# Adding scaled expert rows to x in memory with accumulating scatters

## Chip, cores and metric

The kernel runs on one core of a Trainium2 chip. The metric is the device time of one execution in microseconds (us); for the kernel before, three runs gave 1421.79, 1427.64 and 1428.75, median 1427.64.

## Reference

Two transformer layers on x of shape 8 x 256 x 256 (2048 tokens of 256 values). Six sublayers follow each other, each as `x = layernorm(x + sublayer(x))`; only the last one, a mixture of eight experts with the two best per token, is touched:

```python
gate_scores = softmax(xf @ gate_w)                     # 2048 tokens, 8 experts
topk_scores, topk_idx = top_k(gate_scores, 2)
topk_scores = topk_scores / sum(topk_scores)           # the two shares
h = gelu(einsum('td,edf->etf', xf, w1) + b1)           # 256 -> 1024
y = einsum('etf,efd->etd', h, w2) + b2                 # 1024 -> 256
out = einsum('kt,ktd->td', topk_scores.T, y[topk_idx.T, tok])
x = layernorm(x + out)
```

## The kernel before

**Stages.** A and B (the first two attentions), C (a dense feed-forward), D and E (the second layer's attentions), F (the experts) and a last stage G, each over 8 batches of 256 tokens (two tiles of 128 rows). x stays in SBUF in x_tok. Each engine runs its own program; the order of the work is a list of steps made by in_rounds: an item (first, prio, name, args, at) puts its step k into round first + at[k], and within a round the item that began first comes first. All engines walk the same list and each takes the steps that are its own.

**Routing.** In stage E, at each batch's end (EFIN, SLOTS), the gate gives each token two experts, two shares (set_shares, into the tile shares) and two slots: expert times 2048 plus the token's rank within that expert. GpSimd scatters the token's row of x to x_slots at that slot, and its code (token number, plus 2048 for the second choice) to slot_codes, which was filled with "none" before. SyncE stores x_tok to x_rows as well.

**Experts.** A block is 256 slots of one expert. There are NBK = 23 blocks: the first block of each of the 8 experts, read from x_slots with plain loads, and 15 further blocks, whose expert and rows come from the counts; their weights are gathered by GpSimd (gather_weights, gather_x), three blocks ahead. Slots past an expert's count carry the code "none". Each block has four quarters q = 0 to 3 of its 1024 hidden values, so a round is a quarter, numbered n = 4j + q. Step 0 of a quarter: TensorE computes the hidden values (line 460 to 462 in product), ScalarE applies gelu (L1614) and casts the next weights (split_w, L1585, L1589), VectorE splits the results into a high and a low part (L2010, L2012, w_lo L1935, L1937), GpSimd splits half of the second weights (L761). Step 3: TensorE multiplies by the second weights (L1350), and in the last quarter VectorE adds the bias and leaves the block in yblock (L2021). Step 4, last quarter only: GpSimd scatters the block's 256 rows to y_rows at their codes (L790, two scatters of 128 rows); codes out of bounds are dropped. There are three yblock buffers.

**Codes.** At block 1, quarter 3 (CODES_AT) the codes of all blocks must be known. The last batch's codes are scattered by GpSimd in rounds 0 to 3 (L773); then come a load (first_codes) and a gather (more_codes), a cast of each on VectorE (row_codes, L1950), four transposes on TensorE (L468) and small VectorE steps that give slot_i and token_i.

**Last stage.** When all scatters have landed, SyncE loads y_rows back, two loads of 256 KB a batch (yc). For each batch b in GS, VectorE does four multiply-adds (L2033, share times y plus x) and the layernorm's statistics (ln_stats: L480, L485, L488) in round b, GpSimd a power (L494), VectorE in round b + 2 the scale (L499), ScalarE applies it to two tiles (ln_apply, L508), and SyncE stores the batch. ln_stats waits between L480 and L485 with `dve.wait_ge(s_x[fam], b - 1)`: batch b - 2 must have been applied, since two buffers are shared.

Of the kernel before, what the change touches and what calls it, by code (L numbers as in the profile page):

```python
# [53 lines left out]
def f(ap):  # L54

    return ap.bitcast(F32)
# [100 lines left out]
def f_steps():  # L157
    return in_rounds([(NQ * j + q, 0, "BLK", (j, q), 5 if q == NQ - 1 else 4) for j in range(NBK) for q in range(NQ)])
# [69 lines left out]
def build(nc, a, out):  # L228
    ctx, mid, early, late = ExitStack(), ExitStack(), ExitStack(), ExitStack()
    first_pieces, dw_scope, part, fpart, cpart = (ExitStack() for _ in range(5))  # L230
    with ctx:
# [44 lines left out]
        shares = sb("shares", [P, NT, TOPK])  # L276
# [3 lines left out]
        codes = sb("codes", [P, NT, TOPK], U32)  # L280
# [67 lines left out]
        s_const, s_rtmem, s_none, s_vz = sem("const"), sem("rtmem"), sem("none"), sem("vz")  # L348
# [58 lines left out]
        s_vone, s_shift = sem("ones"), sem("e_shift")  # L407
# [30 lines left out]
        block_codes = [sbf("first_codes", [NE, BT], U32), sbf("more_codes", [NMORE, BT], U32)]  # L438
        block_codes_f = [sbf("first_codes_f", [NE, BT]), sbf("more_codes_f", [NMORE, BT])]
        code_f, token_f = sbf("code_f", [P, BR * NBK]), sbf("token_f", [P, BR * NBK])  # L440
        slot_i, token_i = sbf("slot_i", [P, BR * NBK], U32), sbf("token_i", [P, BR * NBK], U32)
        fpart.close()
        ycs = [sb(f"yc{b}", [P, TOPK, TT, D], F32, cpart, "right") for b in range(B)]
        cpart.close()
# [4 lines left out]
        l_yc = [*((x, 64) for x in (*l_xt, *l_x)), *((x, 128) for x in l_ctx), (l_stage[0], 64), (l_stage[1], 80)]  # L449
# [115 lines left out]
        def set_shares(line, b):  # L565
            r = rt[b % 2]
            line.wait_ge(s_rs, b + 1)
            for t in range(TT):
                made = line.e.tensor_scalar(shares[:, b * TT + t, :], r[:, t, 2, 0:TOPK], r[:, t, 5, 3:4], 1.0, ALU.mult, ALU.mult)
            made.then_inc(s_sh, 1)  # L570
# [27 lines left out]
        def pool_program(pool):  # L598
# [20 lines left out]
            for v in vpad:  # L619
                pool.e.memset(v[:, :, :], 0.0).then_inc(s_vz, 1)  # L620
# [66 lines left out]
            for v in (v_d, *v_e):  # L687
                pool.mark(pool.e.memset(v[:, :, :, DH:32], 0.0))
                pool.wait_own()
                pool.e.memset(v[:, :, :, DH:DH + 1], 1.0).then_inc(s_vone, 1)  # L690
            for name, step, args in DE["pool"]:
# [33 lines left out]
                elif name == "SLOTS" and (args[0] < B - 1 or step < TT):  # L725
                    b, = args
                    pool.wait_ge(w_empty, 16 * (1 + NE))
# [1412 lines left out]
```

## Time and profile before

| | us |
|---|---|
| median of three runs | 1427.64 |
| the profiled execution | 1431.25 |
| its span | 1429.4 |
| TensorE busy | 1290.2 (90%) |
| VectorE busy | 915.3 (64%) |
| GpSimd busy | 730.1 (51%) |
| ScalarE busy | 572.9 (40%) |

In the page and the views PE is TensorE's matmuls, PEld its weight loads, DVE VectorE, ACT ScalarE, POOL GpSimd and SP SyncE; a q behind a name is the engine's queue of instructions. Busy time leaves out waiting and the issue of DMAs by SyncE. A share over the whole span is a mean over very different stages: the rows that matter are those of the expert loop (about 1105 to 1387 us) and of the last stage (1387 us to the end).

### The profile page before, as it was taken

What the parts mean: (1) busy time and instruction counts of PE and PEld (TensorE: products, weight loads), DVE (VectorE), ACT (ScalarE), POOL (GpSimd) and SP (SyncE); (2) the same over time, 40 slices, a digit from 0 to 9 for tenths busy, and PEclk for the clock granted to TensorE, in tenths of its full rate; (3) what the DMA queues carried; (4) which work ended last, traced back from release to release, by engine and by line L of the source; (5) the groups of instructions that cost most, each with busy time, mean ns of one, the idle gap of its engine ahead of it and who ended that gap; (6) DMA issues with size and microseconds to landing.
All of it is one profiled execution on the core that took longest, in us unless ns stands there. A gap on an engine that the chain in (4) does not pass through costs nothing.

```text
span 1429.4 us, 23660 instructions
## 1 busy us (share of the span) xinstructions
PE 1290.2 (90%) x9073; PEld 1098.9 (77%) x9073; DVE 915.3 (64%) x2305; ACT 572.9 (40%) x1172; POOL 730.1 (51%) x697
## 2 busy tenths in 40 slices
PE   6997999999999999999999989998773799999970
PEld 6996788888888888886777767776653799999970
DVE  3665622642272253235688878878765799999966
ACT  3567311121121121113545535544432576777732
POOL 3543566666576666634211242343434347888832
PEclk9998999999999999999999999999875899999995
DMA  6101223233343323310534343434713656666605
GB/s 188 36 22 35 74 89 108 91 115 91 118 133 96 96 88 104 92 62 25 155 93 132 90 81 117 97 88 131 232 43 110 190 198 224 222 231 233 229 18 168
DMA packets 63104, 169.56 MB, mean 119 GB/s; under 512 B 11029, under 2 KB 30735, under 8 KB 55056
## 3 DMA queue, kind: packets, MB, share of 16 engines
q1 hardware_dynamic: 52432, 122.19, 29.1%
q0 software_dynamic: 10560, 45.86, 9.1%
q8 instruction: 72, 1.18, 0.4%
q14 instruction: 40, 0.33, 0.1%
HBM read 138.57 MB, written 33.38 MB: 120 GB/s over the span
## 4 chain that ended last, share of the span: by engine, by line
PE 69%; DVE 16%; issue 4%; DMA 3%; ACT 3%; POOL 3%; SPq 1%; another core or an unknown queue 1%; ACTq 0%; POOLq 0%; DVEq 0%
PE bank L460 15%; PE bank L462 15%; PE bank L461 14%; PE bank L1350 6%; PE bank L468 5%; PE bank L1188 3%; PE bank L1107 3%; DVE shiftE L1873 2%; DVE shiftE L1867 2%; PE bank L1175 2%; PE bank L1266 1%; PE bank L1201 1%; DVE w_lo L1935 1%; DVE gh_hi L2010 1%; DVE x_tok L2033 1%
## 5 line engine op out<-in xcount | busy, mean ns | idle before, releaser
L1733 DVE CAST hid_hi<-bank 128x512 fp32r<-128x512 f32 x96 | 66.4, 691 | 254.9 <-ACT bank L1465 253.8
L602 POOL TENSOR_TENSOR wpiece_lo<-wraw,wpiece_hi 128x1024 fp32r<-128x1024 f32 x88 | 212.3, 2413 | 7.3
L462 PE MATMUL bank<-hid_hi,wpiece_hi 128*128 128x512 f32 x512 | 201.5, 394 | 0.0
L461 PE MATMUL bank<-hid_lo,wpiece_hi 128*128 128x512 f32 x512 | 200.2, 391 | 0.0
L460 PE MATMUL bank<-hid_hi,wpiece_lo 128*128 128x512 f32 x512 | 199.8, 390 | 0.0
L600 POOL TENSOR_SCALAR wpiece_hi<-wraw 128x1024 fp32r<-128x1024 f32 x88 | 93.9, 1067 | 154.4 <-PE bank L462 128.4
L1465 ACT ACTIVATE bank<-bank,ffn_scales 128x512 f32<-128x512 f32 x64 | 42.4, 662 | 304.4 <-PE bank L462 304.4
L461 PEld LDWEIGHTS bank<-hid_lo,wpiece_hi 128*128 128x128 f32 x512 | 96.1, 188 | 22.1
L460 PEld LDWEIGHTS bank<-hid_hi,wpiece_lo 128*128 128x128 f32 x512 | 96.1, 188 | 21.5 <-DVE hid_lo L1735 0.8
L462 PEld LDWEIGHTS bank<-hid_hi,wpiece_hi 128*128 128x128 f32 x512 | 96.2, 188 | 20.0
L460 PE MATMUL bank<-xgT_hi,w_lo 128*128 128x256 f32 x368 | 107.3, 292 | 1.8 <-DVE xgT_lo L1943 1.8
L1614 ACT ACTIVATE bank<-bank,w1raw 128x256 f32<-128x256 f32 x184 | 74.8, 447 | 85.3 <-PE bank L462 84.4
L461 PE MATMUL bank<-xgT_lo,w_hi 128*128 128x256 f32 x368 | 104.4, 284 | 0.0
L462 PE MATMUL bank<-xgT_hi,w_hi 128*128 128x256 f32 x368 | 104.3, 284 | 0.0
L1350 PE MATMUL bank<-w_hi,gh_lo 128*128 128x256 f32 x368 | 103.1, 280 | 0.0
L1350 PE MATMUL bank<-w_hi,gh_hi 128*128 128x256 f32 x368 | 102.8, 279 | 0.0
L1350 PE MATMUL bank<-w_lo,gh_hi 128*128 128x256 f32 x368 | 102.7, 279 | 0.0
L1867 DVE TENSOR_SCALAR_CACHE_REDUCE shiftE<-bank 128x256 f32<-128x256 f32 x256 | 92.9, 419 | 11.2 <-PE bank L1243 8.2
L468 PE MATMUL bank<-ident,shiftE 128*128 128x128 f32 x512 | 72.1, 284 | 24.1 <-DVE shiftE L1873 13.3
L761 POOL TENSOR_TENSOR w_lo<-w2raw,w_hi 128x256 fp32r<-128x256 f32 x92 | 76.4, 846 | 27.9 <-ACT w_hi L1589 27.1
L1873 DVE TENSOR_SCALAR shiftE<-shiftE,topE 128x256 f32<-128x256 f32 x256 | 86.9, 403 | 2.3
L1551 ACT ACTIVATE staging<-bank 128x512 f32<-128x512 f32 x128 | 69.5, 595 | 47.0 <-PE bank L468 38.5
(342 smaller groups left out, 3589.3 us busy)
## 6 DMA issues: line engine op xcount, KB each, us to landing
wraw<-in_C_w SPq DMA_DIRECT2D x88, 512.0 KB, 3.6
w2raw<-in_F_w SPq DMA_DIRECT2D x8, 1152.0 KB, 7.3
w1raw<-in_F_w SPq DMA_DIRECT2D x8, 1028.0 KB, 7.0
split_qk<-qk_hi SPq DMA_DIRECT2D x64, 128.0 KB, 2.7
xt_lo<-split_qk SPq DMA_DIRECT2D x8, 1024.0 KB, 4.8
xt_hi<-split_qk SPq DMA_DIRECT2D x8, 1024.0 KB, 5.3
split_qk<-qk_lo SPq DMA_DIRECT2D x32, 128.0 KB
split_qk<-ctx_raw SPq DMA_DIRECT2D x32, 128.0 KB, 2.4
```

Of the source, the lines that this page charges most:

```text
L460: pe.e.matmul(o, sl, mh, start=start and i == 0, stop=False)
L461: pe.e.matmul(o, sh, ml, start=False, stop=False)
L462: made = pe.e.matmul(o, sh, mh, start=False, stop=stop and i == n - 1)
L468: made = pe.e.transpose(dst, src, ident[0:n, 0:n])
L600: pool.mark(pool.e.tensor_scalar(pair[0], raw, 1.0, 0.0, ALU.mult, ALU.add))
L602: pool.e.tensor_tensor(pair[1], raw, f(pair[0]), ALU.subtract).then_inc(done, 1)
L761: pool.e.tensor_tensor(w2[n % 6][1][:, 1, :], w2_cols(*divmod(n, NQ))[:, 1, :], f(w2[n % 6][0][:, 1, :]), ALU.subtract).then_inc(s_w2lp, 1)
L1350: made = pe.e.matmul(u.ap[:, t * D:(t + 1) * D], hh[:, i, st], ww[:, i, :], start=fc == 0 and k == 0 and t == 0, stop=fc == FC - 1 and k == 2,
L1551: act.e.activation(prob_e[n % 3][:, i, :, :], u.ap[:, :].rearrange("p (k s) -> p k s", k=TT), ACT.Exp, scale=scale_e).then_inc(u.drained, 1)
L1614: made = act.e.activation(u.ap[:, cols], u.ap[:, cols], ACT.Gelu, bias=w1raw[j % 4][:, c:c + 1])
L1867: made = dve.e.tensor_scalar(shift_e[n % 3][:, m, :], scores[:, m, :], lim, -lim, ALU.min, ALU.max, accum_out=top[:, m:m + 1])
L1873: made = dve.e.tensor_scalar(sh, sh, -lim, top[:, m:m + 1], ALU.max, ALU.subtract)
```

## The change

The expert's rows are multiplied by their share while they are in yblock, and added to a copy of x in memory.

- The code of a slot becomes a pair, a mark: code and share. shares, codes and slot_codes give way to marks and slot_marks; set_shares writes into marks. The pairs are scattered, loaded and gathered as before, at twice the size, and the scatter waits for s_sh, the shares. "None" is filled in with two stores instead of one.
- row_codes casts codes and shares apart (four casts), TensorE transposes both (eight transposes), and VectorE makes share_f (the share of each row of each block), token_i, and row_out: the token's row in sum_rows, or a spare row behind the tokens (one for each partition and tile) for slots with no token.
- A new step 4 on ScalarE multiplies the block in place by its shares; step 5, the scatter, adds into sum_rows (compute_op=ALU.add) with no bounds check. Both steps stand 8 rounds behind the block's last quarter, where the scatter stood 4 behind it.
- The scatter of block j waits for the landing of that of block j - 1, since both may add to the same row; that of block 0 waits for the stores of x.
- SyncE stores each batch of x twice, to x_rows and to sum_rows.
- The last stage loads one sum a batch straight into x_tok, and VectorE's multiply-adds are gone.

```diff
 def f_steps():
-    ... "BLK", (j, q), 5 if q == NQ - 1 else 4) ...
+    ... "BLK", (j, q), (0, 1, 2, 3, 8, 8) if q == NQ - 1 else 4) ...
...
-        y_rows = nc.dram_tensor("y_rows", (TOPK * B * S, D), F32, kind="Internal").ap()
+        sum_rows = nc.dram_tensor("sum_rows", (B * S + BT, D), F32, kind="Internal").ap()
-        slot_codes = nc.dram_tensor("slot_codes", (NE * B * S + BT, 1), U32, kind="Internal").ap()
+        slot_marks = nc.dram_tensor("slot_marks", (NE * B * S + BT, 2), U32, kind="Internal").ap()
...
# pool_program
-                elif step == 4:
-                    u = use["F", "y", j]
+                elif step == 5:
                     pool.wait_ge(s_slots, 1)
-                    pool.wait_ge(u.drained, u.done)
+                    pool.wait_ge(s_shared, j + 1)
+                    if j:
+                        pool.wait_ge(w_y[(j - 1) % 3], 16 * BR * ((j - 1) // 3 + 1))
+                    else:
+                        for i in range(2):
+                            pool.wait_ge(w_rows[i], 16 * B)
                     for t in range(BR):
                         pool.e.indirect_dma_start(
-                            y_rows, bass.IndirectOffsetOnAxis(ap=slot_i[:, t * NBK + j:t * NBK + j + 1], axis=0),
-                            ysb[j % 3][:, t, :], None, bounds_check=TOPK * B * S - 1, oob_is_err=False).then_inc(w_y[j % 3], 16)
+                            sum_rows, bass.IndirectOffsetOnAxis(ap=row_out[:, t * NBK + j:t * NBK + j + 1], axis=0),
+                            ysb[j % 3][:, t, :], None, compute_op=ALU.add).then_inc(w_y[j % 3], 16)
...
# sync_program
-                    load(x_rows[b * S:(b + 1) * S, :]..., x_tok[:, b * TT:(b + 1) * TT, :], w_rows[b % 2])
+                    for rows in (x_rows, sum_rows):
+                        load(rows[b * S:(b + 1) * S, :]..., x_tok[:, b * TT:(b + 1) * TT, :], w_rows[b % 2])
...
             for b in range(B):
-                for k in range(TOPK):
-                    load(ycs[b][:, k, :, :], y_rows..., l_yc[b][0])
+                load(x_tok[:, b * TT:(b + 1) * TT, :], sum_rows[b * S:(b + 1) * S, :]..., l_sum[b][0])
...
# scalar_program
+                elif step == 4:
+                    u, marked = use["F", "y", j], use["F", "i"]
+                    act.wait_ge(marked.drained, marked.done)
+                    act.wait_ge(u.drained, u.done)
+                    for t in range(BR):
+                        y = ysb[j % 3][:, t, :]
+                        made = act.e.activation(y, y, ACT.Identity, scale=share_f[:, t * NBK + j:t * NBK + j + 1])
+                    made.then_inc(s_shared, 1)
...
# vector_program, row_codes
                 for k in range(2):
-                    dve.e.tensor_copy(block_codes_f[k][:, :], block_codes[k][:, :]).then_inc(s_codes, 1)
+                    dve.mark(dve.e.tensor_copy(block_marks_f[k][:, 0, :], block_marks[k][:, :, 0]))
+                    dve.e.tensor_copy(block_marks_f[k][:, 1, :], f(block_marks[k][:, :, 1])).then_inc(s_codes, 1)
...
# vector_program, last stage
                 if step == 0:
-                    dve.wait_ge(l_yc[b][0], l_yc[b][1] + 32)
-                    dve.wait_ge(s_x["E"], b + 1)
-                    dve.wait_ge(s_sh, B)
-                    for k in range(TOPK):
-                        dve.wait_own()
-                        for t in range(TT):
-                            n = b * TT + t
-                            made = dve.e.scalar_tensor_tensor(out=x_tok[:, n, :], in0=ycs[b][:, k, t, :], scalar=shares[:, n, k:k + 1],
-                                                              in1=x_tok[:, n, :], op0=ALU.mult, op1=ALU.add)
-                        dve.mark(made)
+                    dve.wait_ge(l_sum[b][0], l_sum[b][1] + 16)
                     ln_stats(dve, "C", B + b, x_tok[:, b * TT:(b + 1) * TT, :])
```

## Rows read from the trace of the kernel before

**Rows 1.** The page, busy time of each engine over the span.

```profile
PE 1290.2 (90%) x9073; PEld 1098.9 (77%) x9073; DVE 915.3 (64%) x2305; ACT 572.9 (40%) x1172; POOL 730.1 (51%) x697
```

**Rows 2.** Windows: stretch, length, busy of PE, PEld, DVE, ACT, POOL, clock, DMA share, GB/s.

```profile
1302.00:1313.60 11.60, 11.60 (x102) 11.60 (x101) 11.46 (x19) 8.12 (x17) 9.98 (x11) 1.00 0.64 239
```

**Rows 3.** Waits of PE, 1085 to 1392: who waited for whom, us, times, longest.

```profile
PE bank L468 <- DVE more_codes_f L1950: 8.7, 1, 8.7
```

**Rows 4.** Chain of waits up to the codes: start us, us, what.

```profile
1112.40 12.09 DMA slot_codes<-codes,slot
...
1125.37 6.88 DMA more_codes<-slot_codes,row_i
...
1132.34 0.28 DVE first_codes_f L1950
...
1132.88 0.60 PE bank L468 x4
```

**Rows 5.** Chain of waits behind the last matmul.

```profile
1386.50 0.70 DVE yblock L2021
...
1387.97 0.97 POOL y_rows L790
...
1389.24 2.10 DMA y_rows<-yblock,slot_i
...
1391.81 3.14 DMA yc<-y_rows
...
1394.97 0.89 DVE x_tok L2033 x2
```

**Rows 6.** Timeline of the last stage: start us, busy us, engine, line, operation [idle before].

```profile
1401.12 1.09 ACT L508 ACTIVATE x_tok<-x_tok,lnC_mv,lnC_rstd 128x256 f32<-128x256 f32 x2 [18.04 <-DVE lnC_mv L499]
...
1403.97 0.15 DVE L499 SCALAR_TENSOR_TENSOR lnC_mv<-lnC_mv,lnC_rstd 128x2 f32<-128x2 f32 x1
1404.04 1.79 DVE L2033 SCALAR_TENSOR_TENSOR x_tok<-yc,shares,x_tok 128x256 f32<-128x256 f32 x4
...
1404.16 1.09 ACT L508 ACTIVATE x_tok<-x_tok,lnC_mv,lnC_rstd 128x256 f32<-128x256 f32 x2 [1.95 <-DVE lnC_mv L499]
1405.86 0.75 DVE L480 BATCH_NORM_STATS2 lnC_stats<-x_tok 128x6 f32<-128x256 f32 x2
1406.65 0.25 DVE L485 BATCH_NORM_AGGREGATE lnC_mv<-lnC_stats 128x2 f32<-128x6 f32 x2
1406.93 0.17 DVE L488 TENSOR_SCALAR lnC_rstd<-lnC_mv 128x2 f32<-128x2 f32 x1
...
1419.37 2.07 ACT L508 ACTIVATE x_tok<-x_tok,lnC_mv,lnC_rstd 128x256 f32<-128x256 f32 x4 [1.95 <-DVE lnC_mv L499]
```

**Rows 7.** Timeline of ACT at the end of the loop.

```profile
1379.48 0.81 ACT L1614 ACTIVATE bank<-bank,w1raw 128x256 f32<-128x256 f32 x2 [1.97 <-PE bank L462]
```

**Rows 8.** Chain of waits ahead of the first block, 1085 to 1140.

```profile
1094.41 4.38 DMA x_slots<-x_tok,slot
1098.88 2.95 DMA xg<-x_slots
```

**Rows 9.** Timeline of DVE behind the codes.

```profile
1137.22 0.69 DVE L2010 CAST gh_hi<-bank 128x512 fp32r<-128x512 f32 x1 [2.72 <-issue]
```

**Rows 10.** Timelines of ACT and of DVE in a block's last quarter.

```profile
1312.24 0.81 ACT L1614 ACTIVATE bank<-bank,w1raw 128x256 f32<-128x256 f32 x2 [0.70 <-PE bank L462]
...
1314.20 0.69 DVE L2010 CAST gh_hi<-bank 128x512 fp32r<-128x512 f32 x1
```

**Rows 11.** Timeline of POOL over one block with gathers.

```profile
1304.47 1.28 POOL L790 DMA_INDIRECT y_rows<-yblock,slot_i  x1 [0.17 <-issue]
1306.06 0.98 POOL L790 DMA_INDIRECT y_rows<-yblock,slot_i  x1 [0.30 <-issue]
...
1311.70 0.96 POOL L739 DMA_INDIRECT w2raw<-in_F_w,wrow_i  x1 [0.35 <-DVE yblock L2021]
...
1316.11 1.28 POOL L790 DMA_INDIRECT y_rows<-yblock,slot_i  x1 [0.17 <-issue]
```

More of the change, by code:

```diff
@@ L229, in build @@
     ctx, mid, early, late = ExitStack(), ExitStack(), ExitStack(), ExitStack()
-    first_pieces, dw_scope, part, fpart, cpart = (ExitStack() for _ in range(5))
+    first_pieces, dw_scope, part, fpart = (ExitStack() for _ in range(4))
     with ctx:
@@ L279, in build @@
         seen = sb("seen", [P, NE], F32R)
-        codes = sb("codes", [P, NT, TOPK], U32)
+        marks = sb("marks", [P, NT, TOPK, 2], U32)
         block_no = sb("block_no", [P, NBK])
@@ L437, in build @@
         wrow_i = sbf("wrow_i", [P, NMORE], U32)
[L438 to L441, printed above, removed]
+        block_marks = [sbf("first_marks", [NE, BT, 2], U32), sbf("more_marks", [NMORE, BT, 2], U32)]
+        block_marks_f = [sbf("first_marks_f", [NE, 2, BT]), sbf("more_marks_f", [NMORE, 2, BT])]
+        code_f, token_f, share_f = (sbf(f"{n}_f", [P, BR * NBK]) for n in ("code", "token", "share"))
+        spare = sbf("spare", [P, BR])
+        row_out, token_i = sbf("row_out", [P, BR * NBK], U32), sbf("token_i", [P, BR * NBK], U32)
         fpart.close()
-        ycs = [sb(f"yc{b}", [P, TOPK, TT, D], F32, cpart, "right") for b in range(B)]
-        cpart.close()
         l_w1, l_w2 = ring(4, lambda i: sem(f"l_w1{i}")), ring(4, lambda i: sem(f"l_w2{i}"))
@@ L735, in pool_program @@
                         else:
-                            pool.e.indirect_dma_start(slot_codes, at, codes[:, b * TT + t, j:j + 1], None).then_inc(w_codes[b % 2], 16)
+                            pool.wait_ge(s_sh, b + 1)
+                            pool.e.indirect_dma_start(slot_marks, at, marks[:, b * TT + t, j, :], None).then_inc(w_codes[b % 2], 16)
             def gather(dst, rows, index, done):
@@ L778, in pool_program @@
                             pool.wait_ge(w_codes[i], 16 * 4 * (B // 2))
-                        gather(block_codes[1][:, :], slot_codes.rearrange("(r s) one -> r (s one)", s=BT), row_i[0:NMORE, 0:1], l_bc)
+                        gather(block_marks[1].rearrange("p s two -> p (s two)"), slot_marks.rearrange("(r s) two -> r (s two)", s=BT), row_i[0:NMORE, 0:1], l_bc)
                     if q == 2 and NE <= j + 3 < NBK:
@@ L831, in sync_program @@
                     load(iota8[:, :], a["iota8"], l_rt)
-                    load(codes[:, :, :], a["codes"], l_rt)
+                    load(marks[:, :, :, :], a["marks"], l_rt)
                     load(block_no[:, :], a["block_no"], l_rt)
@@ L837, in sync_program @@
                     sp.wait_ge(s_none, 1)
-                    load(slot_codes.rearrange("(p n) one -> p (n one)", p=P), none_t[:, :], w_empty)
+                    half = none_t.shape[1]
+                    for i in range(2):
+                        load(slot_marks.rearrange("(p n) two -> p (n two)", p=P)[:, i * half:(i + 1) * half], none_t[:, :], w_empty)
                 elif name == "CTX":
@@ L936, in sync_program @@
                         sp.wait_ge(w_codes[i], 16 * 4 * (B // 2))
-                    load(block_codes[0][:, :], slot_codes[0:NE * B * S].rearrange("(e s) one -> e (s one)", e=NE)[:, 0:BT], l_codes)
+                    load(block_marks[0][:, :, :], slot_marks[0:NE * B * S].rearrange("(e s) two -> e s two", e=NE)[:, 0:BT, :], l_codes)
                 first_weights(j)
@@ L1960, in row_codes @@
                 dve.e.tensor_scalar(token_i[:, :], token_f[:, :], float(B * S - 1), None, ALU.min).then_inc(s_tok, 1)
+                for t in range(BR):
+                    part = slice(t * NBK, (t + 1) * NBK)
+                    made = dve.e.tensor_scalar(row_out[:, part], token_f[:, part], spare[:, t:t + 1], None, ALU.min)
+                made.then_inc(s_slots, 1)
             for n in range(AHEAD - 1):
```

49 lines of the change are left out of this document (27 added, 22 removed).

## The prediction, written before the changed kernel ran

> **What bounds the kernel now.** I read the page first. TensorE is busy for 1290.2 of 1429.4 us [rows 1], so the question is whether the expert loop, which the change edits most, has room for more work. The windows of the loop say that TensorE has none to give: it is busy for all 11.60 us of a stretch as long as one block of 256 rows, at the full granted clock, with VectorE at 11.46, ScalarE at 8.12 and GpSimd at 9.98 [rows 2]. Work added there costs nothing as long as it does not make TensorE wait. Before the loop runs full there is one stall that bounds it: TensorE waits 8.7 us for the row codes in block 1 [rows 3]. It ends a chain in which the last scatter of codes lands 12.09 us after its issue starts, the gather of the codes takes 6.88, and a cast and four small transposes follow [rows 4].
>
> Behind the last matmul comes the tail, on which no TensorE work lies. In the chain of waits [rows 5] VectorE ends the last y block at 1387.20, GpSimd starts its two scatters at 1387.97 and 1389.24, the second has landed at 1391.34, the first loads at 1394.95. Then the last layernorm runs, batch by batch, at the pace of the ScalarE pairs in the timeline: 1401.12, 1404.16, so 3.04 us a batch [rows 6]. ScalarE ends at 1421.44 (1419.37 and 2.07). The rest, 8.0 us to the span's end, are the last stores and fixed steps; I leave it as it is.
>
> **The change, part by part.** The sum is against the profiled execution: 1431.25 us with a span of 1429.4. Its median neighbour is 1427.64, 3.6 lower (0.25%), and I add the difference to that. I call L the time from the start of the second scatter of a block to the landing of both.
>
> *Layernorm stage.* Each batch loses four VectorE multiply-adds (1.79 us a batch [rows 6]). What is late next? Not VectorE alone. In ln_stats the aggregation of batch b waits until ScalarE has applied batch b-2, and that starts right behind the scale at the head of the same round. Today the multiply-adds cover it. From rows 6: a scale's ScalarE pair starts 0.04 us behind its end, so some 0.19 behind its start, and takes 1.09; then aggregation (0.25), 0.03 gap, the add of epsilon, and the next scale starts 0.08 behind that add's start. So 0.19+1.09+0.05+0.28+0.08 = 1.7 us a round. Rounds 0 and 1 have no such wait: statistics 0.75, aggregation 0.25, add 0.17 and gaps, 1.24 each. The end after the last round stays 2.15 (26.47 us of stage less 8 x 3.04, rounded). So 2.5+6x1.7+2.15 = 14.85 against 26.47 (1394.97 to 1421.44): 11.6 saved. The other end, if the wait turned out free, is 1.24 a round, 2.8 more.
>
> *Loads.* One 256 KB load instead of two stands ahead of the first batch, which takes away the second issue, 0.4 us. The other seven arrive in time: the sixteen of today never stopped VectorE after the first batch.
>
> *The scatters at the end.* Here lies the price. Steps 4 and 5 are now 8 rounds behind the block's last quarter instead of 4, and each scatter waits for the landing of the one before. So block 20 is shared on ScalarE only behind the gelu that starts at 1379.48 and ends at 1380.29 [rows 7]; two 128x256 activations take at most the 1.09 of the layernorm pair, so 1381.4. GpSimd starts 0.77 later, as in rows 5, and its second scatter 1.27 behind the first: 1383.4. Landed at 1383.4+L. Block 21 waits for that. From a landing to GpSimd's next issue it took 0.88 us (12.09 behind 1112.40 is 1124.49, next issue 1125.37 [rows 4]), and again 1.27 to the second: 1385.55+L, landed at 1385.55+2L. Block 22 likewise: its second scatter starts at 1387.7+2L, landed at 1387.7+3L. Its own data (VectorE 1387.20, ScalarE 1388.3) would allow 1390.3, which is earlier for any L over 1.3. Against 1391.34 this costs 3L-3.64.
>
> L is what the trace does not show. The nearest rows: the last scatter today, 2.10 [rows 5]; a plain scatter of 128 full 1 KB rows in quiet traffic, 4.38, and a 256 KB load from the same memory, 2.95 [rows 8]; a scatter of codes in the burst of weight loads, 12.09 [rows 4]. The 2.10 is a floor, not a neighbour: counted on these inputs, the routing fills 21 of the 23 blocks, so blocks 21 and 22 are padding, whose rows the bounds check drops today, and which the new kernel writes to spare rows. An accumulate also reads its destination. Bounds in quiet traffic: 2.10, and 4.38+2.95 = 7.33 if read and write go one behind the other. I take 5.4, the plain scatter plus a third of the read, since I expect the rows of one scatter to overlap. The tail's scatters then cost 3x5.4-3.64 = 12.6.
>
> *Codes become marks.* The scatter has as many descriptors, of 8 bytes for 4; the gather reads 2 KB for 1 KB in each of 15 rows. I cost both at nothing, hidden in 12.09 and 6.88 [rows 4], which for transfers this small are waits and not bytes; the far bound is a few tenths. VectorE makes four casts for two (0.28 alone, some 0.21 in a row: +0.45), TensorE eight transposes for four (0.60 [rows 4]: +0.6). Both stand behind the gather and ahead of TensorE: +1.05, bounds 0.5 and 1.6. The further VectorE steps (a copy, two adds, two minima for one cast, about 1 us) fit in its idle 2.72 us ahead of the next cast of gh_hi [rows 9].
>
> *Loop.* ScalarE gets one pair of at most 1.09 us a block, ahead of the weight casts of the block's last quarter. Its idle time ahead of a gelu there is 0.70, so the gelu comes up to 0.4 late; VectorE takes that quarter up at 1314.20, 1.1 us behind the gelu's end at 1313.05 [rows 10]. Nothing. GpSimd's scatter no longer waits for the y block, but for the landing of the one before. In a block with gathers its second scatter starts at 1306.06 and the next block's first at 1316.11 [rows 11], so less the 0.88 wake-up a landing within 9.2 us is free. The weight gathers stand ahead in the queue; the DMA share of 0.64 [rows 2] says that they are drained 7.4 us behind their start, some 2 us into this span. Nothing at L = 5.4, but see the rivals. The second copy of x rows (eight stores, the last beside a store at 1080), the second fill, and the waits for s_sh, long met, are off the path: SyncE and the queues wait there for the slots anyway. They cost nothing; without that cover a 256 KB store is some 3 us.
>
> Sum: -11.6-0.4+12.6+1.05 = +1.6, or as a formula 3L-14.6. On 1427.64 that is 1429.2 us. The layernorm's gain is spent on three scatters in single file.
>
> *What the Trainium skill says of it.* The three landings stand in file because each scatter waits for the one before. The Trainium skill ("DMA: Bandwidth & Descriptors", Rules for kernel authors) says that an accumulating DMA beside another access of the same bytes can lose an addition, and to wait for the earlier one's semaphore; so overlapping them is no way out. No row here shows it. The same page (Anatomy of one DMA) puts a DMA issued by GpSimd at 2.0 us plus bytes over 436 GB/s; as an estimate 2.3 us for 128 KB. The sum by it would be -7.7. The 4.38 of [rows 8] disagrees.
>
> **The rivals.**
> A landing near the floor (faster). If a written and added row costs little over a dropped one, L is 2.1 to 2.5: -8.3 to -7.1, and with the 1.24 us rounds down to -11.1: 1417 to 1420. For it: 2.10 is the only row of this very instruction. Against it: those rows carry no data, and the scatter that does took 4.38 [rows 8]. The Trainium skill's fit for one DMA, named above, would lead here.
>
> A slow landing in the tail (slower). Place: the three serial scatters. It decides from L = 7.3, where 3L-14.6 passes 7. At 7.33 the price is +7.4, and halfway to the 12.09 of rows 4, at 9.7, it is +14.5: 1435 to 1442. For it: three landings each multiply the unknown. Against it: the tail's traffic is quiet.
>
> A landing that blocks GpSimd in the loop (slower). GpSimd has no spare time in a gather block: from 1304.47 to 1316.11 it waits only 0.35 us for a y block, the other gaps are its own issue gaps [rows 11]. At 12.09 a landing comes 2.9 us too late in each of the 15 gather blocks. The weight halves are split some four rounds (11 us) before TensorE needs them, and 15 x 2.9 = 44 us of lag would have to eat that first; the pace of yblock and gathers takes back part. I price it at +10 to +30 with the tail. It decides from a landing over 9.2 us in traffic. Against it: the queue is drained early in the span.
>
> The layernorm doesn't shorten (not what the change says). If stores and loads, now closer together, set the pace at 2.5 us a batch for 1.7, 8 x 0.8 = 6.4 us are lost: +8. Today's sixteen loads, at half the distance, speak against it.
>
> **How the numbers follow.** Forecast (L from 2.6 to 7.2) 0.48, 1429.2, with its own range 1421 to 1435; floor 0.19; slow landing in the tail 0.18; GpSimd blocked 0.12; no shorter layernorm 0.03. 0.5% is 7.1 us, about what a measurement of this kernel can tell from no change. So faster 0.19, same 0.48, slower 0.33. The range reaches down to the floor with free rounds (1417) and up to a landing of 9.7 (1442), with 2 us for the loop: 1417 to 1444.
>
> **What would show it.** In the chain of waits of the new kernel, three scatters into sum_rows follow each other behind 1383, with GpSimd idle and released by a DMA; their length is L, and every us off 5.4 moves the time by 3. The ScalarE pairs of the last stage come 1.7 us apart, 3.04 before. The wait for the marks is about 1 us longer. GpSimd's waits for a scatter inside the loop are zero, and TensorE's windows stay at 11.6. The forecast is wrong if a scatter lands outside 2.6 to 7.2 us, if the last scatters overlap, or if GpSimd shows DMA waits between 1178 and 1350.

## The result, and the profile after

The changed kernel takes 1416.98 us (median of 11 runs, 1411.14 to 1423.05) where the kernel before takes 1425.15 on the same chip (1420.74 to 1428.98): a ratio of 0.9943, 95% interval 0.9927 to 0.996. In a second comparison (after2, below) it is 0.9954 (0.9932 to 0.9976). The forecast was 1429.2, no change (+1.6), and a range whose low end is 1417.0; the time fell just under it. Against the kernel before on the same chip it is 8.2 us, or 0.57%, faster. The profiled execution of the changed kernel took 1413.02 us.

To see where the time went I cut both traces at the same events: the first transpose of an expert block, the end of the last yblock, and the end. The kernel before reaches the first event at 1101.87, the second at 1387.20 [rows 5], the end at 1429.4. The changed kernel: 1082.52, 1374.52, 1410.7. So ahead of the experts it gains 19.4 us (the forecast had nothing there), in the expert loop it loses 6.7 (291.99 against 285.33), behind it it gains 6.1 (36.2 against 42.2). Of the 19.4 a part is chance; the experiments say how much.

The first rows are TensorE's waits from 1085 to 1392, as in [rows 3]: who waited for whom, us in total, times, longest.

```profile
PE bank L458 <- DVE xgT_lo L1957: 10.7, 14, 1.4
PE bank L466 <- DVE more_marks_f L1965: 4.1, 1, 4.1
```

The wait for the codes is 4.1 us where it was 8.7, and another has grown: TensorE waits 10.7 us in 14 waits for xgT_lo, VectorE's half of the next block's rows, where it waited 1.8 us in two. Windows over one block with gathers, to be read beside [rows 2] (length, busy PE, PEld, DVE, ACT, POOL, clock, DMA share, GB/s):

```profile
1317.60:1330.00 12.40, 11.99 (x104) 11.79 (x102) 12.26 (x19) 9.21 (x20) 10.61 (x12) 1.00 0.77 223
```

A block takes 12.4 us here; TensorE is idle for 0.4 of them, where it had no idle time in 11.60. GpSimd over the same block, to be read beside [rows 11]:

```profile
1312.33 1.88 POOL L793 DMA_INDIRECT sum_rows<-yblock,row_out  x1 [0.17 <-issue]
1314.52 1.92 POOL L793 DMA_INDIRECT sum_rows<-yblock,row_out  x1 [0.30 <-issue]
1315.89 2.69 POOL L760 TENSOR_TENSOR w_lo<-w2raw,w_hi 128x256 fp32r<-128x256 f32 x3
1318.74 1.26 POOL L738 DMA_INDIRECT w1raw<-in_F_w,wrow_i  x1 [0.16 <-issue]
1320.53 0.98 POOL L738 DMA_INDIRECT w2raw<-in_F_w,wrow_i  x1 [0.53 <-DVE yblock L2044]
...
1324.97 1.89 POOL L793 DMA_INDIRECT sum_rows<-yblock,row_out  x1 [0.17 <-issue]
```

Issuing an accumulating scatter holds GpSimd for 1.9 us; the plain one held it 1.28 and 0.98. From scatter to scatter it is 12.64 us, and again GpSimd has no gap but its own issue gaps and 0.53 us of wait. VectorE at that time:

```profile
1314.30 0.68 DVE L1949 TENSOR_TENSOR w_lo<-w1raw,w_hi 128x512 fp32r<-128x512 f32 x1
...
1316.55 2.58 DVE L1949 TENSOR_TENSOR w_lo<-w1raw,w_hi 128x512 fp32r<-128x512 f32 x1
```

The same instruction takes 0.68 us while GpSimd issues a scatter (1314.52 to 1316.44), and 2.58 while it works off its three splits (1315.89 to 1318.58). The Trainium skill ("SBUF — State Buffer", Who interferes with whom) says that a VectorE instruction with two SBUF inputs contends with a GpSimd instruction that reads SBUF; these two are such a pair, and the trace agrees. No run here takes one of the two away.

The end of the chain of waits, beside [rows 5]:

```profile
1370.57 4.02 DMA sum_rows<-yblock,row_out
...
1374.63 0.69 issue
1375.33 1.55 POOL sum_rows L793
1376.88 0.30 issue
1377.18 3.66 DMA sum_rows<-yblock,row_out
1380.88 0.69 issue
1381.57 1.54 POOL sum_rows L793
1383.11 0.30 issue
1383.41 3.77 DMA sum_rows<-yblock,row_out
```

These are the three scatters in single file that the forecast drew. L is 4.02, 3.66 and 3.77, not 5.4. The last stage, ScalarE's timeline, beside [rows 6]:

```profile
1398.11 1.09 ACT L506 ACTIVATE x_tok<-x_tok,lnC_mv,lnC_rstd 128x256 f32<-128x256 f32 x2 [0.65 <-DVE lnC_mv L497]
1399.85 1.09 ACT L506 ACTIVATE x_tok<-x_tok,lnC_mv,lnC_rstd 128x256 f32<-128x256 f32 x2 [0.65 <-DVE lnC_mv L497]
```

1.74 us a batch, 3.04 before.

One more stretch is shorter. From ScalarE's last end to the end of the span it was 8.0 us (1421.44 to 1429.4), and now it is 5.3 (1405.40 to 1410.7).

### The profile page after: what moved, and what is told of

It is laid out like the page before. It is cut to its first block, busy times and chain, and to the rows that moved or that the text cites. A ratio compares the mean times of both kernels' runs of the same rounds, so it can differ in the third digit from the quotient of the medians.

```text
span 1410.7 us, 23667 instructions
## 1 busy us (share of the span) xinstructions
PE 1282.1 (91%) x9077; PEld 1091.3 (77%) x9077; DVE 915.0 (65%) x2279; ACT 593.0 (42%) x1218; POOL 751.6 (53%) x697
## 4 chain that ended last, share of the span: by engine, by line
PE 60%; DVE 23%; issue 6%; POOL 3%; ACT 3%; DMA 3%; SPq 1%; ACTq 0%; DVEq 0%; POOLq 0%
PE bank L458 14%; PE bank L460 13%; PE bank L459 13%; DVE w_lo L1949 5%; PE bank L466 5%; PE bank L1193 3%; PE bank L1112 3%; DVE gh_hi L2033 3%; PE bank L1356 2%; DVE shiftE L1887 2%; DVE shiftE L1881 2%; PE bank L1180 2%; DVE w_lo L1951 2%; PE bank L1206 2%; PE bank L1271 1%
## 5 line engine op out<-in xcount | busy, mean ns | idle before, releaser
L1471 ACT ACTIVATE bank<-bank,ffn_scales 128x512 f32<-128x512 f32 x64 | 42.4, 662 | 304.4 <-PE bank L460 304.4
L458 PE MATMUL bank<-xgT_hi,w_lo 128*128 128x256 f32 x368 | 108.2, 294 | 10.7 <-DVE xgT_lo L1957 10.7
L1949 DVE TENSOR_TENSOR w_lo<-w1raw,w_hi 128x512 fp32r<-128x512 f32 x92 | 99.1, 1077 | 0.0
L793 POOL DMA_INDIRECT sum_rows<-yblock,row_out x46 | 81.4, 1770 | 32.4 <-ACT yblock L1628 13.2
L760 POOL TENSOR_TENSOR w_lo<-w2raw,w_hi 128x256 fp32r<-128x256 f32 x92 | 81.9, 1120 | 29.2 <-ACT w_hi L1595 28.8
```

What stands on the lines that cost most here:

```text
L458: pe.e.matmul(o, sl, mh, start=start and i == 0, stop=False)
L760: pool.e.tensor_tensor(w2[n % 6][1][:, 1, :], w2_cols(*divmod(n, NQ))[:, 1, :], f(w2[n % 6][0][:, 1, :]), ALU.subtract).then_inc(s_w2lp, 1)
L793: pool.e.indirect_dma_start(sum_rows, bass.IndirectOffsetOnAxis(ap=row_out[:, t * NBK + j:t * NBK + j + 1], axis=0), ysb[j % 3][:, t, :], ...
L1949: dve.e.tensor_tensor(w1[n % 4][1][:, :, :], w1_cols(j, q), f(w1[n % 4][0][:, :, :]), ALU.subtract).then_inc(s_w1lo, 1)
```

## The experiments

The experiments ran on four chips, and these are of two kinds: on two of them the kernel before takes 1425 to 1426 us (the first kind, as the chip of the result), on the other two it takes 1406 (the second kind). Ratios are to the kernel before on the same chip, with 95% intervals. "Start" is the first transpose of an expert block, "loop" the stretch from there to the end of the last yblock, "tail" the rest of the span.

| kernel | kind of chip | ratio | start | loop | tail |
|---|---|---|---|---|---|
| before | first | | 1101.9 | 285.3 | 42.2 |
| before2 | first | | 1095.0 | 283.5 | 42.7 |
| before3 | second | | 1077.7 | 283.0 | 42.2 |
| changed | first | 0.9943 (0.9927 to 0.996) | 1082.5 | 292.0 | 36.2 |
| after2 | first | 0.9954 (0.9932 to 0.9976) | 1088.1 | 291.1 | 35.5 |
| m8 | second | 0.9966 (0.995 to 0.9983) | 1079.5 | 277.8 | 42.1 |
| m8b | second | 0.9953 (0.9936 to 0.997) | 1073.7 | 279.3 | 42.2 |
| m8c | first | 0.9871 (0.9843 to 0.9898) | 1087.5 | 279.4 | 42.2 |
| addr, addr2 | second | 1.0001 (0.9985 to 1.0018) | 1074.9, 1080.0 | 283.1, 283.1 | 42.3, 42.2 |
| addr3 | first | | 1099.9 | 283.5 | 42.4 |
| noacc | second | 0.9915 (0.9889 to 0.9941) | 1074.4 | 282.5 | 32.4 |
| noshare | first | 0.9943 (0.9924 to 0.9961) | 1086.9 | 292.9 | 34.8 |
| at4 | second | 0.9975 (0.996 to 0.9991) | 1080.0 | 297.0 | 30.3 |
| late | first | 0.9901 (0.9866 to 0.9936) | 1087.6 | 292.9 | 30.5 |
| best | second | 0.9945 (0.9926 to 0.9965) | 1079.5 | 293.9 | 27.3 |
| bestb | first | 0.9881 (0.9856 to 0.9907) | 1085.0 | 294.8 | 27.4 |
| best2 | first | 0.99 (0.9877 to 0.9924) | 1085.1 | 281.6 | 40.1 |

**The wider codes alone.** m8 is the kernel before with the marks of 8 bytes (with their second fill and the wait for the shares) and nothing else of the change:

```diff
-        slot_codes = nc.dram_tensor("slot_codes", (NE * B * S + BT, 1), U32, kind="Internal").ap()
+        slot_marks = nc.dram_tensor("slot_marks", (NE * B * S + BT, 2), U32, kind="Internal").ap()
...
-   pool.e.indirect_dma_start(slot_codes, at, codes[:, b * TT + t, j:j + 1], None)
+   pool.e.indirect_dma_start(slot_marks, at, marks[:, b * TT + t, j, :], None)
```

> The kernel before with one part of the change: a slot's code becomes a pair of 8 bytes (code and share), filled, scattered, loaded and gathered as in the changed kernel; the shares that come along are not used, y_rows, the multiply-adds and the scatter of the blocks stay. In the two traces the first expert block starts at 1101.87 before and 1082.52 after, and the wait for the codes is 8.7 before and 4.1 after, both ahead of any accumulate. Theory W (the width of the scattered elements does it: 4-byte scatters land late and hold up other DMAs of stage E): this kernel is 8 to 20 us faster than before, the codes' wait is near 4, GpSimd's wait for the last codes near 5 and not 11. Rival V (chance from run to run, or something else of the change): within 3 us of before, and the wait for the codes stays near 8.7.

Measured 0.9966, 4.9 us, less than the 8 to 20 that the theory named, and more than chance would give. The wait for the codes is 3.6 us and GpSimd's wait for the last codes 4.7 (7.4 to 8.7 and about 10 to 11 in the traces with 4-byte codes). The loop is 277.8 us against 283. The first rows are GpSimd's waits in the kernel before, the second those of m8c, both of the stretch 1070 to 1380:

```profile
POOL more_codes L739 <- DMA slot_codes<-codes,slot: 10.9, 1, 10.9
```

```profile
POOL more_codes L739 <- DMA slot_marks<-marks,slot: 4.8, 1, 4.8
```

So part of the change's gain is a scatter whose elements are twice as large and land 6 us sooner. Beside addr on the same chip (1074.9) the start did not come earlier (1079.5), which left the 19 us open.

**The place of the tensors in memory.** addr moves y_rows behind split_qk in the kernel before:

```diff
-        y_rows = nc.dram_tensor("y_rows", ...)
         split_qk = ring(2, lambda i: nc.dram_tensor(f"split_qk{i}", ...))
+        y_rows = nc.dram_tensor("y_rows", ...)
```

> The kernel before with the tensor y_rows declared behind split_qk, so that split_qk and what lies behind it move in memory by 4 MB. The change also moves tensors in memory (sum_rows is smaller than y_rows). Theory W (width of the scattered elements) expects no difference beyond 2 us here, and the wait for the codes at 8.7. Rival A (the place of split_qk and slot_codes in memory sets the time of stage E): a difference of 5 us or more in either direction, with the start of the first expert block moved.

1.0001: no effect. The wait for the codes is 7.6 us.

**Second traces on a chip of the first kind.**

> The kernel before once more, for a second trace. Theory: 8 us of the first trace's stage E were chance (all engines stood still from 852 to 856), so the first expert block starts at 1070 to 1090 here, the wait for the codes is again 7.5 to 9, GpSimd's wait for the last codes 10 to 11, 283 to 285 us from the first expert block to the last yblock, 42.2 from there to the end. Rival: stage E of the kernel before is slow in every trace, and it starts at 1095 or later.

> The changed kernel once more, beside the kernel before on the same chip, for a second trace. Theory: stretches that the change does not touch move from trace to trace (the first expert block starts at 1101.87 in one trace of the kernel before, at 1074.9 in the trace of addr, and at 1082.52 in that of the changed kernel), while the parts it touches repeat: TensorE's wait for the marks 4 us (7.6 to 8.7 with 4-byte codes), 290 to 293 us from the first expert block to the end of the last yblock (283 to 285 before), 36 us from there to the end (42.2 before). The ratio is 0.992 to 0.998. Rival: the early start of the experts belongs to the change; then it starts 10 us or more ahead of the kernel before here too.

The parts that the change touches repeat (loop 283.5 and 291.1, waits 8.2 and 4.0). The start comes at 1095.0 and 1088.1, 6.9 us apart where it was 19.4, so a part of the 19.4 was chance. But the second expectation's rival is not dead, and what I had called chance in before2's expectation was not: batch 2 of stage E again took 56.3 us. These are the stores of x at its two ends in the two traces of the kernel before, then in the changed one (SyncE's timeline: start, us):

```profile
831.29 0.38 SPq L799 DMA_DIRECT2D x_rows<-x_tok  x1
887.56 0.38 SPq L799 DMA_DIRECT2D x_rows<-x_tok  x1
```

```profile
828.62 0.38 SPq L799 DMA_DIRECT2D x_rows<-x_tok  x1
884.94 0.38 SPq L799 DMA_DIRECT2D x_rows<-x_tok  x1
```

```profile
829.73 0.38 SPq L802 DMA_DIRECT2D x_rows<-x_tok  x1
878.52 0.38 SPq L802 DMA_DIRECT2D x_rows<-x_tok  x1
```

56.3, 56.3 and 48.8 us. Windows of the kernel before show what happens in between, and GpSimd's timeline what comes just ahead:

```profile
848.18 1.03 POOL L736 DMA_INDIRECT slot_codes<-codes,slot  x1 [0.17 <-issue]
849.52 0.95 POOL L736 DMA_INDIRECT slot_codes<-codes,slot  x1 [0.30 <-issue]
```

```profile
848.00:852.00 4.00, 4.00 (x37) 2.39 (x37) 1.85 (x9) 1.66 (x6) 2.00 (x3) 1.00 1.80 88
852.00:856.00 4.00, 0.90 (x7) 0.66 (x7) 0.00 (x0) 0.00 (x0) 0.00 (x0) 0.99 0.41 49
856.00:860.00 4.00, 1.94 (x9) 2.03 (x10) 3.46 (x21) 1.49 (x3) 1.39 (x6) 0.50 0.35 71
```

A pair of 4-byte scatters goes out, the DMA share of the window is 1.80 (packets that overlap for long) at only 88 GB/s, and then VectorE, ScalarE and GpSimd do nothing at all for 4 us, TensorE nearly nothing, and its granted clock is at the lower of its two levels (0.50) when it resumes. In every kernel with 8-byte marks this share is under 0.9, and no engine stops. The long packets are not those of the scatters: from 850 to 860 the queue of the scatters has a share of 0.4%, that of SyncE's stores of split_qk 52.9%. The trace gives no releaser in the program for the waits of VectorE and ScalarE (GpSimd waits for VectorE in turn):

```profile
POOL route L560 <- DVE route L1908: 8.1, 1, 8.1
ACT feat L1517 <- remote: 7.0, 1, 7.0
DVE v_e L1782 <- remote: 6.4, 1, 6.4
```

**Does it follow the width, the place, or the chip?**

> The kernel before, a third trace. In two traces of it (before, before2) batch 2 of stage E takes 56.3 us between the stores of x (831.29 to 887.56, 828.62 to 884.94) and all engines stand still some 2 to 4 us behind GpSimd's second pair of 4-byte scatters; in addr, also with 4-byte scatters, it takes 48.8, as in every kernel with 8-byte scatters. Theory W: the 4-byte scatters hold the DMA engines (their share is 1.4 to 1.8 there against 0.6 to 0.9) and may stop the engines, on one chip and not on another; then before3 and addr2 on one chip behave alike. Rival A: the place in memory decides; then before3 shows 56.3 and addr2 48.8 on the same chip.

> The kernel addr (4-byte codes, y_rows declared behind split_qk) once more, beside before3 on one chip. Theory W: batch 2 of stage E takes as long as in before3. Rival A: 48.8 whatever before3 shows.

> The kernel m8 (only the codes widened to 8 bytes) once more. Theory W: batch 2 of stage E takes 48.8, the DMA share behind the second pair of scatters is under 1, TensorE's wait for the codes 3.6 to 4; the ratio to the kernel before is 0.9966 on a chip where the kernel before shows no standstill, and 0.988 to 0.992 on one where it does (8 us of standstill and up to 6 of the codes' wait). Rival: 0.9966 on any chip, and the standstill is chance.

All three fell on a chip of the second kind. before3 and addr2 both take 48.8 us for batch 2 with a share of 1.73 and 1.53, so this kind has the long packets without the standstill; m8b is 0.9953, as m8. On a chip of the first kind m8c and addr3 settled it:

> The kernel m8 (only the codes widened to 8 bytes) on a further chip. On a chip where the kernel before takes about 1425 us, both its traces show batch 2 of stage E at 56.3 us; on one where it takes about 1406, three traces with 4-byte codes show 48.8. Theory W: on a 1425 us chip this kernel shows 48.8, starts the first expert block near 1088 (1095 to 1102 in the kernel before) and has a ratio of 0.988 to 0.992; on a 1406 us chip 0.995 to 0.997 as in m8 and m8b. Rival: the ratio is 0.996 on both, and the gain of the changed kernel ahead of the experts on the 1425 us chip comes from another part of the change.

> The kernel addr (4-byte codes, y_rows declared behind split_qk) once more. Theory W: on a 1425 us chip batch 2 takes 56.3 us, as in before and before2. Rival A (the place of the tensors in memory decides on that chip): 48.8.

m8c has 0.9871, 18.1 us, at the gaining end of what was expected and beyond it. Its batch 2 takes 48.8 us, its share in the window of the scatters is 0.86, at 196 GB/s:

```profile
848.00:852.00 4.00, 4.00 (x38) 2.64 (x37) 3.85 (x20) 1.97 (x8) 2.66 (x3) 1.00 0.86 196
```

addr3, with 4-byte codes in another place of memory, takes 56.7 us (833.36 to 890.03) and starts at 1099.9. So on this kind of chip the width of the scattered codes alone moves the start, and the place in memory has no part in it: three traces with 4-byte codes start at 1095.0 to 1101.9, seven with 8-byte codes at 1082.5 to 1088.1, with means 12.8 us apart. On the second kind three traces with 4-byte codes start at 1074.9 to 1080.0 and five with 8-byte codes at 1073.7 to 1080.0, no difference. What the engines stand still for is not shown, since the trace says only "remote". Nor is it shown why the second kind does not stop.

**The accumulate.** noacc is the changed kernel with plain scatters:

```diff
-                            ysb[j % 3][:, t, :], None, compute_op=ALU.add).then_inc(w_y[j % 3], 16)
+                            ysb[j % 3][:, t, :], None).then_inc(w_y[j % 3], 16)
```

> The changed kernel with plain scatters of the blocks into sum_rows, which leaves the adding out: a row holds the last writer's values. In the changed kernel a scatter of a block holds GpSimd for 1.55 us (1.9 beside VectorE's work) against 0.97 to 1.28 before, a block with gathers takes 12.4 to 12.6 us against 11.64, and TensorE waits 10.7 us for xgT_lo. Theory: the accumulate itself makes the issue longer, and that makes the loop longer: here the issue is back at about 1.0 to 1.3, blocks take 11.65, TensorE's wait for xgT_lo is under 3, and the kernel is 8 to 12 us faster than the changed one. Landing time of a scatter: 3.8 in the changed kernel; if the adding costs little, 3.3 to 3.8 here as well, if it costs a read, under 3. Rival (the activation with the shares on ScalarE is what makes the loop longer): blocks stay at 12.5.

The loop is 282.5 us, blocks take 11.64, the wait for xgT_lo is 2.5, VectorE's w_lo is back at 0.87 us mean (1.09 in the changed kernel). GpSimd's issues of these scatters are at 1.08 us mean against 1.77. The changed kernel has no trace on a chip of this kind, but best, which also adds, has a loop of 293.9 there. So the adding costs the loop 9 to 11 us. The edit takes away the longer issue and the longer landing together; that it is the issue is read from GpSimd's waits, where a landing comes up once inside the loop. That noacc is 8 to 12 us faster than the changed kernel is not measured, as the two ran on different kinds of chip. The landing, from the chain:

```profile
1355.53 0.96 POOL sum_rows L793
1356.79 2.36 DMA sum_rows<-yblock,row_out
1359.90 0.96 POOL sum_rows L793
1361.16 2.38 DMA sum_rows<-yblock,row_out
```

2.37 us with all 128 rows written, so the padding has no part in L: what was left open as "a floor for dropped rows" is the plain landing. The accumulate adds 1.3 to 1.7 us to the landing and 0.6 to the issue. The expectation's first arm on the landing (3.3 to 3.8 if adding costs little) missed, the second (under 3) held.

noacc also parts the stretch behind ScalarE's last end. It is 8.0 us there, as in all eleven traces without adding, where the seven with it have 5.2 to 5.3. So the adding gives back 2.7 us at the very end; why, no run shows.

**ScalarE's share of it.** noshare cuts the multiplication down to one element.

```diff
-                    for t in range(BR):
-                        y = ysb[j % 3][:, t, :]
-                        made = act.e.activation(y, y, ACT.Identity, scale=share_f[:, t * NBK + j:t * NBK + j + 1])
-                    made.then_inc(s_shared, 1)
+                    y = ysb[j % 3][:, 0, 0:1]
+                    act.e.activation(y, y, ACT.Identity, scale=share_f[:, j:j + 1]).then_inc(s_shared, 1)
```

> The changed kernel with the activation that multiplies a block by its shares cut down to one element, which leaves the shares out of the sum. Theory (the accumulate's longer issue on GpSimd makes the loop longer, not ScalarE): VectorE's w_lo L1949 stays near 1.08 us mean (0.88 before and in noacc), TensorE's wait for xgT_lo near 10 us, the loop near 292 us. Rival (ScalarE's extra pair delays the gelu and with it VectorE): the loop falls to 284.

Loop 292.9, w_lo 1.053 mean, wait for xgT_lo 10.7, ratio 0.9943 (after2 on the same chip: 0.9954): the activation costs nothing that these runs can tell, as forecast.

**The single file at the end.** at4 has lag 4 in place of 8 in all blocks, late only in the last three.

```diff
-    ... (0, 1, 2, 3, 8, 8) if q == NQ - 1 else 4) ...          # changed kernel
+    ... (0, 1, 2, 3, 4, 4) if q == NQ - 1 else 4) ...          # at4
+    ... ((0, 1, 2, 3, 8, 8) if j < NBK - 3 else (0, 1, 2, 3, 5, 5) if j == NBK - 3
+         else (0, 1, 2, 3, 4, 4)) if q == NQ - 1 else 4) ...   # late
```

> The changed kernel with the sharing and the scatter 4 rounds behind a block's last quarter instead of 8. Theory: the end is set by three scatters in file (issue of the first at 1368.72, landed 1387.21). Four rounds earlier block 20 and 21 land before the last matmul, and block 22 issues at about 0.7 us behind its activation: landed 12.0 to 12.8 us... measured from the end of the last yblock, 7.3 us instead of 12.7, so the tail is 5 to 6 us shorter. In the loop ScalarE now waits for yblock ahead of its weight casts; if that costs nothing the kernel is 5 us faster than the changed one, if it delays each last quarter by up to 1 us, the loop eats it (0 to 10 us slower there). Rival (the file of scatters is not what sets the end): the tail stays at 36 us from the last yblock to the end.

> The changed kernel with only the last three blocks shared and scattered earlier (block 20 five rounds, 21 and 22 four rounds behind the last quarter, the others eight as before). In at4 the end came 30.3 us behind the last yblock instead of 36.2, but the stretch from the first expert block to there took 297 us instead of 292. Theory: the lag of 4 rounds in every block costs the loop, the file of scatters costs the end, and they are separate: here 30.3 us at the end and 292 in the loop, 5 to 6 us faster than the changed kernel. Rival: the 297 of at4 are chance, and this kernel is as fast as at4.

at4's tail is 30.3 us, as expected (5.9 less), but its loop is 297.0, so the whole gains little (0.9975). late keeps both, 30.5 and 292.9, and has 0.9901, 5.6 us less than after2 on the same chip. That the lag of 4 costs the loop 3 to 5 us (293.9 in best on this kind of chip, 292 in the changed kernel) is one trace; why, I did not test.

**A third buffer.** best is late with a third set of statistics in the last stage, so that the aggregation waits for batch b - 3:

```diff
-            dve.wait_ge(s_x[fam], b - 1)
+            dve.wait_ge(s_x[fam], b - (2 if fam == "C" and b >= B else 1))
```

> The kernel late with a third buffer of layernorm statistics in the last stage, so that the statistics of batch b wait for batch b - 3 and not b - 2. Theory: the 1.74 us from batch to batch in the last stage are scale, ScalarE's pair (1.09) and the wait of the aggregation for it; with a third buffer the pace is VectorE's own, 1.3 us, and 6 rounds save 2.6 us. So 0.4 us less per round, 27.7 us from the last yblock to the end (30.3 in late), ratio 0.988 (late had 0.9901). Rival (loads or stores set the pace): 1.74 stays, and VectorE waits for the loads or the stores end later.

> The kernel best once more, beside best2 and m8c on one chip. Theory: 27.3 us from the last yblock to the end, 291 to 293 in the loop; ratio 0.994 on a 1406 us chip, 0.987 to 0.989 on a 1425 us chip, so slower than best2 by 8 us.

Tail 27.3 and 27.4. VectorE's statistics in best now follow each other at 1.21 us, with no wait:

```profile
1387.22 0.74 DVE L482 BATCH_NORM_STATS2 lnC_stats<-x_tok 128x6 f32<-128x256 f32 x2
...
1388.43 0.74 DVE L482 BATCH_NORM_STATS2 lnC_stats<-x_tok 128x6 f32<-128x256 f32 x2
```

So the 1.74 us were the wait for ScalarE. 0.9945 on a chip of the second kind missed the 0.988 expected, which I had worked out from late on the first kind; there bestb has 0.9881, as expected. Its loop of 294.8 is over the 291 to 293 expected, and it is not slower than best2 by 8 us, but level with it (1409.0 and 1410.8).

**Without accumulates, but with the rest.** best2 keeps marks, shares on ScalarE and three buffers, scatters plainly to y_rows, and lets GpSimd add a batch's two rows.

```diff
+                pool.e.tensor_tensor(y0, y0, y1, ALU.add).then_inc(s_both, 1)
...
+                    dve.mark(dve.e.tensor_tensor(xb, xb, ycs[b][:, 0, :, :], ALU.add))
```

> 8-byte marks and shares applied on ScalarE in the loop as in the changed kernel, but plain scatters to y_rows with the bounds check and no waits among them, the last blocks early as in late, and in the last stage GpSimd adds a batch's two rows, VectorE adds the sum to x and makes the statistics, with three buffers. Theory: the loop has no accumulates and takes 277 to 279 us as in m8 (291 to 293 in the changed kernel). In the last stage the pace is GpSimd's, one addition of 128x512 (1.3 us, as qk_lo L713) and a power (0.7): 2.0 to 2.3 us a batch against 3.04 in the kernel before and 1.21 in best, so 34 to 36 us from the last yblock to the end. That makes 0.987 on a 1406 us chip and 0.980 to 0.985 on a 1425 us chip. Rival: GpSimd and VectorE slow each other in the last stage, 2.8 us a batch or more, 0.991 on a 1406 us chip.

The loop came out near expectation (281.6), the tail not: 40.1 for 34 to 36. GpSimd's power takes 1.19 us there, 0.69 in the changed kernel, so a batch takes 2.53 us, half way to the rival. The ratio is 0.99 where 0.980 to 0.985 was expected: no better than bestb.

On the first kind of chip m8c (0.9871) and bestb (0.9881) both beat the changed kernel (0.9943 and 0.9954), on the second m8 and m8b (0.9966, 0.9953) and best (0.9945) lie together. Both have the wide codes. bestb pays for the adding in the loop (294.8 against 279.4) and has it back in the tail (27.4 against 42.2); the two sums are 322.2 and 321.6. No run has the short loop and the short tail together. Nor did the changed kernel itself run on the second kind, where the wide codes do not move the start. Taking from best what early scatters and the third buffer gave (5.6 and 3.2 us) leaves it, as an estimate, at a ratio of about 1.000 there, no gain.

## Why the prediction was wrong

**The time ahead of the experts: marks "hidden in 12.09 and 6.88".** This is the step that failed. The forecast looked at the marks as at bytes (8 for 4), costed scatter and gather "at nothing", and bounded the cost at "a few tenths", above nothing only. The price was negative. GpSimd's wait for the last codes fell from between 9.9 and 10.9 us to between 4.2 and 5.2, TensorE's from between 7.4 and 8.7 to between 3.1 and 5.3, and on chips of the first kind a standstill that made a batch 7.5 us longer went too. m8 and m8c show that the width alone does it: m8c takes 18.1 us less than the kernel before. The row was there to be read: a scatter of 128 elements of 4 bytes took 12.09 us [rows 4] and one of 128 rows of 1 KB 4.38 [rows 8]. I put the difference down to the burst of weight loads and did not ask whether it was the elements.

**Codes, on VectorE and TensorE: +1.05.** About right: four casts stand 0.2 us apart and eight transposes take 0.67 us, where four took 0.60 [rows 4], so the transposes cost 0.1 and not 0.6, together about +0.5, the lower bound.

**Loop: "Nothing".** This step failed too, by 12 us the other way: 291.1 to 292.0 against the 279.4 of m8c, the kernel with about the same wait for the codes. The forecast wrote itself that GpSimd has no spare time in a gather block, and then priced only the wait for a landing, not a longer issue. The issue is 1.9 us instead of 1.28 and 0.98, 1.5 us a block, in the engine that had none to spare. The rival about GpSimd named the place and the victim (TensorE, through late halves) and the wrong reason: inside the loop it waits once for a landing, 3.0 us at 1135.88, and never between 1178 and 1350, though one landing took 9.2 us, outside the 2.6 to 7.2 that the forecast set as its sign. noacc shows that the adding does it; that it does it by its issue, and that VectorE's w_lo is the link between GpSimd and xgT_lo, is read from the rows, not shown by a run.

**The scatters at the end.** The mechanism was right, block by block. L was mis-sized: 3.8 for 5.4. A step of the file, from issue to issue, is 6.24 us (1375.33 to 1381.57), the forecast had 7.55; a part of the smaller landing (1.6) went into the longer issue (0.58). Landed at 12.7 us behind the last yblock, forecast 16.7, which is 4.0 us of the tail's miss. The plain landing is 2.37 and not 4.38; [rows 8] was the last of a file of scatters, and in quiet traffic the row to take was the 2.10 of [rows 5], which I had put aside as a floor for dropped rows. The Trainium skill's fit for one DMA ("DMA: Bandwidth & Descriptors", Anatomy of one DMA), which the forecast had set against 4.38, gives an estimate of 2.3 us for 128 KB: the trace of noacc agrees, with 2.37 for the plain scatter, and the accumulate lies 1.4 over it.

**Layernorm stage.** Right in mechanism and size: 1.74 us a batch (forecast 1.7), from the first statistics to ScalarE's end 15.4 us (14.85). Not all loads arrived in time, as the forecast had it: the third batch waited 0.9 us for its own. In after2 it did not, and the stage took 15.0. best confirms which wait it is.

**Behind ScalarE's end: "I leave it as it is".** The term was put at nothing and was worth 2.7 us: 8.0 before, 5.3 after. noacc, with 8.0, shows that it comes with the adding. How, is open.

Put together for chips of the first kind, two traces each: start 1098.4 to 1085.3, loop 284.4 to 291.6, tail 42.4 to 35.8: -13.1, +7.2, -6.6, in sum -12.5, where the medians say -8.2 and -7.5. The two traces of the kernel before differ by 8.2 us, those of the changed one by 4.2. The forecast's terms for the same: 0, +1.05, +0.6. So the forecast missed three stretches by 13, 6 and 7 us, and the loop's loss hides a part of the rest. That the time ends so close to the stated range is luck: its low end belongs to the rival with L of 2.1 to 2.5, and L was 3.7 to 4.0.

## What to carry to other kernels

Price the issue of an instruction and not only its landing, on the engine that issues it, and look whether that engine has a gap; an accumulating scatter held GpSimd for 1.9 us here where a plain one held it for 1.0 to 1.3. Ask of a slow transfer of tiny elements whether the element size is its reason, before putting it down to its neighbours, and try that part of a change by itself: on chips of the first kind the widened codes alone are worth more than the whole change. And compare kernels on one chip: the kernel before took 1406 us on some chips and 1425 on others, and what the codes' width was worth differed with it (0.9966 and 0.9871).

## What the runs showed of the hardware

- The last of four scatters of 128 elements of 4 bytes landed 12 us behind its issue, where the 8-byte one took about 6 (from the last issue at 1093.07 to the load behind it at 1099.58 in the changed kernel), under the same weight loads, and the DMA share behind a pair of them was 1.3 to 1.8 against 0.6 to 0.9. With 4-byte scatters TensorE stood still for 2.9 to 4.1 us, and VectorE, ScalarE and GpSimd for 6.3 to 8.9, on chips of the first kind in three traces of three, and on the second kind in none of three.
- A plain scatter of 128 rows of 1 KB: 0.97 us of issue, 2.37 to landing. The same with an add in memory: 1.54 (1.9 in the loop) and 3.6 to 4.0. With such adds the span ended 5.2 to 5.3 us behind ScalarE's last instruction in seven traces, and 8.0 in the eleven without.
- VectorE's w_lo took 0.68 us while GpSimd issued an accumulating scatter, and 2.58 while it ran its splits.
- Rows that a bounds check drops (2.10 us) save only 0.3 us against rows that are written (2.37).
